# A fused attention and mixture-of-experts kernel: normalisings move from VectorE to ScalarE, lo parts from GpSimd to VectorE, and short chains are laid around the row maxima

## The reference

```python
# x: 16 x 512 x 512, ctx: 16 x 512 x 1024, 16 heads of 32
k, v = split(ctx, 2, axis=2)
q = layernorm(x) * 32 ** -0.5
w = softmax(q_heads @ k_heads.T + b + mask(lens))
x1 = x + tanh(g_xattn) * (w @ v_heads)

z = layernorm(x1)
gates = softmax over the top 2 of 8 of (cosine(z, centroids) + z @ w_route.T)
h = gelu(z @ w1[e] + b1[e])                       # for the 8 experts
x2 = x1 + tanh(g_ffn) * sum_e gates[e] * (h @ w2[e] + b2[e])
```

## Time and profile before

| what | value |
|---|---|
| time, median of 3 runs | 2116.63 us (2108.9 to 2117.64) |
| the profiled execution: its own time | 2109.41 us |
| its span | 2107.5 us |
| PE busy | 1874.4 us, 89% |
| DVE busy | 1521.0 us, 72% |
| ACT busy | 1123.6 us, 53% |
| POOL busy | 652.6 us, 31% |
| mean granted TensorE clock | 0.97 |

### The profile page before, as it was taken

One profiled execution on the slowest core, in us unless ns is written; L12 is line 12 of the kernel. 1 busy time (PEld: TensorE's weight loads), 2 busy tenths in 40 slices (PEclk: granted clock), 3 DMA queues, 4 the chain that ended last, 5 costly groups with the idle time before them and its releaser, 6 DMA issues. The chain is left out here.

```text
span 2107.5 us, 38543 instructions
## 1 busy us (share of the span) xinstructions
PE 1874.4 (89%) x10720; PEld 1050.3 (50%) x10721; DVE 1521.0 (72%) x3639; ACT 1123.6 (53%) x2044; POOL 652.6 (31%) x547
## 2 busy tenths in 40 slices
PE   0599999999999999999999999999459898998987
PEld 0344444444444444444444444444347777777775
DVE  6578788877878777787787787874366666666665
ACT  0165556556555564655655556565145555555554
POOL 1112112111111111211111111210057777777776
PEclk9999999999999999999999999999679999999999
DMA  3877777777876777776887777772348877887774
GB/s 110 134 121 154 115 177 144 136 158 118 187 146 125 156 118 172 141 139 147 134 182 141 130 155 125 154 136 92 124 88 155 145 152 133 159 143 135 140 149 71
DMA packets 173114, 292.01 MB, mean 139 GB/s; under 512 B 37982, under 2 KB 42078, under 8 KB 172944
## 3 DMA queue, kind: packets, MB, share of 16 engines
q1 hardware_dynamic: 140016, 222.26, 52.1%
q0 software_dynamic: 32928, 67.68, 18.4%
HBM read 127.09 MB, written 71.63 MB: 94 GB/s over the span
## 5 line engine op out<-in xcount | busy, mean ns | idle before, releaser
L918 DVE TENSOR_REDUCE mx<-bank 128x1 f32<-128x512 f32 x1024 | 692.8, 685 | 240.2 <-PE bank L714 225.0
L622 ACT ACTIVATE prob<-bank 128x512 f32<-128x512 f32 x1024 | 577.7, 595 | 484.7 <-PE bank L702 484.6
L590 POOL TENSOR_TENSOR regrouped_then_w<-regrouped_then_w 128x512 fp32r<-128x512 f32 x128 | 165.3, 1291 | 1146.6 <-ACT regrouped_then_w L612 1146.6
L714 PE MATMUL bank<-stA,stB 98*128 98x512 f32 x1024 | 427.4, 420 | 71.2 <-DVE mx L918 42.1
L702 PE MATMUL bank<-stB,stA 100*128 100x512 f32 x1024 | 467.5, 459 | 9.1 <-issue 8.8
L702 PEld LDWEIGHTS bank<-stB,stA 100*128 100x128 f32 x1024 | 196.4, 193 | 207.9 <-ACT prob L622 117.0
L675 PE MATMUL bank<-prob,vin 128*32 128x512 f32 x2048 | 279.0, 617 | 0.0
L675 PE MATMUL bank<-prob,ones 128*32 128x512 f32 x2048 | 278.6, 617 | 0.0
L714 PEld LDWEIGHTS bank<-stA,stB 98*128 98x128 f32 x1024 | 202.5, 198 | 117.5 <-DVE mx L918 72.0
L1184 POOL DMA_INDIRECT out_dram<-yout,scatter_ids x144 | 227.8, 1582 | 53.4 <-issue 53.4
L1116 PE MATMUL bankb<-w_hi,gelu_parts 128*128 x576 | 199.4, 407 | 47.9 <-DVE gelu_parts L1358 47.9
(11 more groups left out here) (184 smaller groups left out, 2162.3 us busy)
## 6 DMA issues: line engine op xcount, KB each, us to landing
stB<-regrouped_then_w SPq DMA_DIRECT2D x192, 256.0 KB, 5.7
stA<-regrouped_then_w SPq DMA_DIRECT2D x192, 256.0 KB, 8.4
x_k_then_w<-in_x_dram SPq DMA_DIRECT2D x16, 1024.0 KB, 6.5
x_k_then_w<-in_ctx_dram SPq DMA_DIRECT2D x16, 1024.0 KB, 9.1
vin<-in_ctx_dram SPq DMA_DIRECT2D x16, 1024.0 KB, 6.3
xres<-in_x_dram SPq DMA_DIRECT2D x16, 1024.0 KB, 14.1
xn_rows<-xn SPq DMA_DIRECT2D x64, 256.0 KB, 2.3
out_dram<-xres SPq DMA_DIRECT2D x16, 1024.0 KB, 10.2
```

The costliest lines, as they stand in the source:

```text
L590: pool.tensor_tensor(turnedL[:, side, :], turned[:, side, :], turnedH[:, side, :].bitcast(F32), ALU.subtract).then_inc(s_lo, 1)
L622: act.activation(prob[:, u % 2, j, :], psS[j % 2][:, :], ACT.Exp).then_inc(s_exp, 1)
L714: pe.matmul(psM[s % 2][:, :], stB[0:98, g, j, i * P:(i + 1) * P], stA[0:98, g, j, :], start=True, stop=True).then_inc(s_m, 1)
L918: dve.tensor_reduce(mx[:, s // 4, s % 4:s % 4 + 1], psM[s % 2][:, :], AX.X, ALU.max).then_inc(s_mx, 1)
```

## The change

`turned` and POOL's subtraction go. ACT copies each turned tile once, rounded, and DVE subtracts it from the bank itself (`lo_part`, slots 1 and 5). Both normalisings become ACT instructions with scale and bias from SBUF, each with one more short DVE operation for the bias (`shift`, `shift2`): that of Q in slots 7, 9, 12 and 14 of the step with g 0, that of x1 one step later than before, in slot 8. Turning x1 moves to slot 10 and the routing product to slot 14. The multiplication by tanh(g_xattn) is folded into the addition to `xres`, and the scaling is done in place in the PSUM bank. The two chains for 1/sqrt are put two operations to a slot, one on either side of the maximum: `row_scale` in slots 0 to 8 of the step with g 1, `scale` in slots 5 to 12 of the step with g 3. Column aggregation moves to slots 14 and 15, the statistics of x to steps with g 2 and 3. SP loads `xres` at the end of its step rather than ahead of the rows.

```diff
-TURNS = [("TQ", 3), ("XT", -5), ("MT", 1), ("TK", 3), ("DT", -1), ("OT", -1), ("LG", -5)]
+TURNS = [("TQ", 3), ("MT", 1), ("TK", 3), ("DT", -1), ("OT", -1), ("XT", -5), ("LG", -5)]
...
 SP
-                        if st.on(0):
-                            ...
-                            sp.dma_start(xres[:, par, :, :], x_d[bass.ds(b, 1)]...).then_inc(s_res[par], 16)
...
-                    if st.on(-4):
-                        sp.wait_ge(s_xn2, st.count(1, -4, 1))
+                    if st.on(-5):
+                        sp.wait_ge(s_xn2, st.count(1, -5, 1))
...
+                    if st.g() == 0 and st.on(0):
+                        ...
+                            sp.wait_ge(s_xn2, st.count(1, -4, 0))
+                        sp.dma_start(xres[:, par, :, :], x_d[bass.ds(b, 1)]...).then_inc(s_res[par], 16)
...
 POOL
-                    if st.on(3):
-                        for side, name in ((0, "TQ"), (1, "TK")):
-                            ...
-                            pool.tensor_tensor(turnedL[:, side, :], turned[:, side, :], turnedH[:, side, :].bitcast(F32),
-                                               ALU.subtract).then_inc(s_lo, 1)
...
 ACT
+                def normalise(st):
+                    i, par, half = st.g(-5), ((st.l + 3) // 4) % 2, (st.l + 1) % 2
+                    act.wait_ge(s_ln2, st.batch(LN2, -5, ROW_READY))
+                    ...
+                    act.activation(xn2[:, half, :], xres[:, par, i, :], ACT.Identity, bias=shift2[:, i:i + 1],
+                                   scale=rsb[:, i:i + 1]).then_inc(s_xn2, 1)
+                def normalise_q(st, i):
+                    ...
+                    ins = act.activation(xg[:, i, :].rearrange("p (g c h) -> p g h c", g=NG, h=HG),
+                                         xin[:, par, i, :].rearrange("p (g h c) -> p g h c", g=NG, h=HG),
+                                         ACT.Identity, bias=shift[:, par, i:i + 1], scale=rstd[:, par, i:i + 1])
...
-                    act.activation(turned[:, side, :], bank[:, :], ACT.Copy).then_inc(s_full, 1)
-                    act.activation(turnedH[:, side, :], bank[:, :], ACT.Copy).then_inc(took, 1)
+                    act.activation(turnedH[:, side, :], bank[:, :], ACT.Copy).then_inc(s_full, 1)
...
+                        if s == 8 and st.on(-5):
+                            normalise(st)
+                        if s == 11 and st.on(-5):
+                            bank, took = take_turn(act, st, "XT")
+                            ...
+                        if st.g() == 0 and s in (7, 9, 12, 14) and st.on(4):
+                            normalise_q(st, (7, 9, 12, 14).index(s))
...
 PE
-                        if s == 1 and st.on(-5):
+                        if s == 10 and st.on(-5):
                             pe.wait_ge(s_xn2, st.count(1, -5, 1))
                             bank, done = put_turn(pe, st, "XT")
...
-                        if s == 9 and st.on(-5):
+                        if s == 14 and st.on(-5):
                             b, before = turn_of(st, "XT")
...
 DVE
+                def row_scale(st, k):
+                    c = lambda k: st.batch(LN2, -5, k)
+                    if k == 0:
+                        dve.wait_ge(s_ln2, c(6))
+                    if k < RSQRT_STEPS:
+                        rsqrt(dve, rsb[:, :], rst[:, :], varb[:, :], s_ln2, lambda k: c(6 + k), k, k + 1)
+                        return
+                    ...
+                def lo_part(st, side):
+                    dve.wait_ge(s_full, st.count(2, 3, side + 1))
+                    bank, took = take_turn(dve, st, "TK" if side else "TQ")
+                    dve.tensor_tensor(turnedL[:, side, :], bank[:, :], turnedH[:, side, :].bitcast(F32),
+                                      ALU.subtract).then_inc(took, 1)
...
                     for s in range(16):
+                        if st.g() == 1 and s <= 8 and st.on(-5):
+                            row_scale(st, 2 * s)
+                        if st.g() == 3 and 5 <= s <= 12 and st.on(5):
+                            scale(st, 2 * (s - 5))
                         if st.on(2):
                             ... the maximum of slot s
+                        if s == 0 and st.on(-6):
+                            route_logit(st, s)
+                        if st.g() == 1 and s <= 8 and st.on(-5):
+                            row_scale(st, 2 * s + 1)
+                        if st.g() == 3 and 5 <= s <= 12 and st.on(5):
+                            scale(st, 2 * (s - 5) + 1)
-                        if st.g() == 0 and 1 <= s <= 4 and st.on(4):
-                            normalise_q(st, s - 1)
...
+                        if s in (1, 5) and st.on(3):
+                            lo_part(st, s // 5)
...
-                            dve.tensor_scalar(rsum[:, :, :], rsum[:, :, :], tanh_a[:, 0:1], None, ALU.mult).then_inc(s_rsum, 1)
...
-                            dve.tensor_tensor(scaled[:, :, :]..., bank[:, :]..., each, ALU.mult).then_inc(took, 1)
+                            dve.tensor_tensor(heads, heads, each, ALU.mult).then_inc(s_scaled, 1)
...
-                            dve.tensor_tensor(dst, dst, scaled[:, :, :], ALU.add).then_inc(s_x1a, 1)
+                            dve.scalar_tensor_tensor(out=dst, in0=bank[:, :]..., scalar=tanh_a[:, 0:1],
+                                                     in1=dst, op0=ALU.mult, op1=ALU.add).then_inc(took, 1)
...
-                    if st.on(-4):
-                        if st.g() == 0:
-                            ln2(st, 16)
-                        normalise(st)
```

More of the change, by code:

```diff
@@ L234, in flamingo_kernel @@
             kg = w2a[:, NT * D:2 * NT * D].rearrange("p (i d) -> p i d", i=NT)
[L235 to L236 removed]
+            turnedH, turnedL = [w2a[:, 2 * NT * D + 2 * S * t:2 * NT * D + 2 * S * (t + 1)].rearrange("p (a s) -> p a s", a=2)
+                                        for t in range(2)]
             turnedH, turnedL = turnedH.bitcast(F32R), turnedL.bitcast(F32R)
@@ L624, in step @@
                             evac_turned(st, s // 4)
-                        if s == 1 and st.on(-5):
-                            bank, took = take_turn(act, st, "XT")
-                            act.activation(xT[:, :, :].rearrange("p k t -> p (k t)"), bank[:, :], ACT.Copy).then_inc(took, 1)
                         if s == 3 and st.on(1):
@@ L641, in step @@
                             act.activation(dst[:, (st.l + 1) % 2, :], src[:, :], ACT.Copy).then_inc(s_out, 1)
+                        if s == 8 and st.on(-5):
+                            normalise(st)
+                        if s == 11 and st.on(-5):
+                            bank, took = take_turn(act, st, "XT")
+                            act.activation(xT[:, :, :].rearrange("p k t -> p (k t)"), bank[:, :], ACT.Copy).then_inc(took, 1)
+                        if st.g() == 0 and s in (7, 9, 12, 14) and st.on(4):
+                            normalise_q(st, (7, 9, 12, 14).index(s))
                         if s == 10 and st.g() == 1 and st.on(-6):
@@ L722, in step @@
                             turn_rows(st, s // 4)
-                        if s == 1 and st.on(-5):
-                            pe.wait_ge(s_xn2, st.count(1, -5, 1))
-                            bank, done = put_turn(pe, st, "XT")
-                            for k in range(KD):
-                                last = pe.transpose(bank[:, k * P:(k + 1) * P], xn2[:, (st.l + 1) % 2, k * P:(k + 1) * P], ident[:, :])
-                            last.then_inc(done, 1)
                         if s == 3 and st.on(1):
@@ L742, in step @@
                             last.then_inc(done, 1)
-                        if s == 9 and st.on(-5):
+                        if s == 10 and st.on(-5):
+                            pe.wait_ge(s_xn2, st.count(1, -5, 1))
+                            bank, done = put_turn(pe, st, "XT")
+                            for k in range(KD):
+                                last = pe.transpose(bank[:, k * P:(k + 1) * P], xn2[:, (st.l + 1) % 2, k * P:(k + 1) * P], ident[:, :])
+                            last.then_inc(done, 1)
+                        if s == 14 and st.on(-5):
                             b, before = turn_of(st, "XT")
@@ L809, in ln2 @@
                         dve.reciprocal(nrm[:, 2, :], nrm[:, 1, :]).then_inc(s_ln2, 1)
-                def normalise(st):
-                    i, par = st.g(), ((st.l + 4) // 4) % 2
-                    dve.wait_ge(s_ln2, st.batch(LN2, -4, LN2))
-                    if st.rnd is not None or st.l - 4 >= 2:
-                        dve.wait_ge(s_xns[st.l % 2], st.pair(16, -4, 0))
-                    dve.tensor_scalar(xn2[:, st.l % 2, :], xres[:, par, i, :], mvb[:, i, 0:1], rsb[:, i:i + 1],
-                                      ALU.subtract, ALU.mult).then_inc(s_xn2, 1)
```

142 lines of the change are left out of this document (72 added, 70 removed).

## The result

| what | before | after |
|---|---|---|
| time, median | 2112.92 us (2108.90 to 2117.64) | 2054.91 us (2054.68 to 2057.13) |
| the profiled execution / its span | 2109.41 / 2107.5 us | 2054.78 / 2052.4 us |

What follows compares the result with a forecast made beforehand. PE was taken as nearly the bound, at 20.26 us a free step. Gains of 61.4 us in the loop, 6.8 and 3.8 outside, less 1, gave 71: profiled 2109.4 to 2038, median 2040, range 2024 to 2062.

Steps and rivals of the forecast that it cites:

- rival B: DVE late around slot 9: in-place scaling and addition cost 0.86 us, 0.3 us a step, time 2060; chance 0.14.
- The two stalls: Late maxima in steps with g 0 and where g 1 begins: both go, 3.98 us × 12 batch elements = 47.8 us.
- It is part of the 3.98 us, not extra: Wait for stA rows in steps with g 0, 5.7 us: removing it adds no gain beyond the stalls'.
- The 'issue' wait … stays: PE's wait where the loop body begins anew, five times: stays at 8.8 us, plus 8.5 us of half clock.
- I cost this at nothing: SP's new load order: stack rows come sooner, though the step is 4 us shorter; no cost counted.
- The clock behind the stalls: Stretches at half clock behind the DVE stalls in the loop go, a gain of 18.4 us.
- Load on DVE: About no change per step; lateness around slots 8 and 9 costs 1 us for the whole kernel, bound 19 us.
- Rival A: Lo part of K, on DVE, is held under POOL's K copy: 41 us less gain, time 2081; chance 0.05.
- Rival C: ACT alternating exponential and Identity loads tables at each change: 192 us net, time 2230; chance 0.03.
- Rival D: The loop's beginnings no longer bring half clock: 8.5 us more gain, time 2031; chance 0.1.
- my reason: PE's turnings cost 0.44 us behind a plain product, 0.39 behind a PV; moving two loses 4.8 us.
- The tail and the first steps: Outside the loop: 3.2 and 0.6 us gained in the tail, 6.8 us in two more batch elements.

Runs made afterwards that it cites:

- e4: Kernel before with only the multiplication by tanh folded into the addition to xres: 2090.10 us, ratio 0.9893.
- e9: Kernel before with the tanh multiplication folded into the addition and xres loaded at the end of SP's step: 2077.71 us, ratio 0.9848.
- e10: Kernel before with only the lo parts moved to DVE and ACT copying each turned tile once: 2108.55 us, ratio 0.9988.
- e3: Kernel before with the store of the normalised tile moved behind the loads of x and K, so these precede the jump: 2118.13 us, ratio 1.0037.
- e2: Kernel after with x loaded at the end of SP's step with g 0 and K at the end of that with g 1: 2035.05 us, ratio 0.9637.
- e1: Kernel after with the loads of x and K held until the logits of the step before are done: 2052.41 us, ratio 0.9716.
- e7: Kernel after with a loop body of 16 steps in place of 8: 2031.84 us, ratio 0.9622.
- e8: Kernel after with x and K loaded in separate steps away from the jump and a body of 16 steps: 2027.88 us, ratio 0.9605.
- e11: Kernel after with x and K loads spread, a body of 16 steps, and the turning of x1 one slot later, behind a PV product: 2038.29 us, ratio 0.9667.
- e5: Kernel after with the lo parts taken back: ACT copies each turned tile twice and POOL subtracts: 2064.24 us, ratio 0.9780.
- e6: Kernel after with Q normalised by ACT without the permutation, so the attention is not the reference's: 2056.68 us in one execution.

## Why the prediction was right, and where it was off

**The number: inside the range, by luck in part.** 2054.91 us lies in 2024 to 2062 and outside the 2030 to 2050 that I gave to my own forecast. The upper end is rival B's, a late DVE, and that didn't come. What filled the place up to it was a cost that no rival named.

**The two stalls: right.** 47.8 us were to go; PE's wait for maxima is gone, and between jumps three steps of four take 20.37 us, within 0.01 of the predicted floor of 20.36; the fourth, with g 3, takes up to 20.56, and these 0.13 to 0.19 us, twelve times, are the 1 us or so that I took for DVE's lateness, and a little more. e4, e9 and e10 show that it took the parts together: the fold frees the K copy's place (e4), SP's order frees the rows that come next (e9), and the lo parts pay only once the normalising of Q has left DVE (e10). "It is part of the 3.98 us, not extra" was right for the rows, in the earlier trace rows; that they would become the longer wait once the maxima were gone, had SP's order not changed, the prediction did not say.

**"The 'issue' wait … stays": the term that failed.** I took it over unchanged, 8.8 us and 8.5 us for the clock. It is 20.5 and 13.3, and that is 16.5 of the loop's shortfall of 16.8 us. The prediction had the cause in hand: "it reaches the loads of x and K half a step earlier, over a step whose DMA share is low" and "I cost this at nothing". I asked only whether the rows would come late, and not what else stands in the DMA engines' queues at that moment. e3 shows the size in the kernel before (8.8 to 22.9 us), e2 in the kernel after (20.5 to 7.1), e1 that the fetch of each engine counts, and e7 that it goes with the number of jumps.

**The clock behind the stalls: right in the event, not shown as caused.** I took 18.4 us for half clock behind DVE's stalls. In the trace after, half clock stands at the jumps alone, as forecast. But e3 has none away from its jumps either, and 37.9 us of stalls for maxima. So the stalls don't bring half clock each time, and how much of the 18.4 us the change itself gave back is open.

**Load on DVE: right.** PE has no new wait in slots 10 to 13, so rival B is out (its weight loads wait in slot 13, 3.3 us in all); the operations that no row had shown cost 0.70 and 0.74 us, of the bounds 0.54 and 0.86.

**ACT: price wrong, conclusion right.** 0.59 us for a normalising came from a copy out of PSUM. It costs 0.80, and 1.32 with the permutation. ACT is 657.88/48 = 13.7 us a step where I wrote less than 12.7, and it had the room. At the start it had not: four normalisings in front of the first product take 4.42 us together, 2.40 on DVE before, 2.0 more, and the first part is 1.8 us longer.

**Rival A: false for its victim.** The lo part of K is not held, and neither is the inversion, both with a PSUM operand. **Rival C: false.** Still two table loads in the whole run, one in the setup and one in the expert part, 1.28 us each; identity alternates with the exponential in every step. **Rival D**, a clock kept after the loop's beginnings, didn't come with the kernel after; e2 and e8 come close to it, once the loads are moved.

**PE: the sum right, its reason not shown.** Slot 10 takes 0.93 and slot 14 1.35 us, 0.46 and 0.88 more than a plain one. The step's sum came out within 0.01 us. By my reason a turning behind a PV is cheaper. e11 moved one there and lost 0.1 us a step, but it took slack from DVE at the same time, so it doesn't tell the price by itself.

**The tail and the first steps: undersized.** 3.51 us a tile and 6.2 us in all against 3.69 and 3.8; steps −2 to 7 gained 6.9 us and not half of it, and the waits for rows in them, which I had not counted, fell from 7.7 to 5.6 us together, and 3.4 us of half clock at 192.8 us are gone. The rest of both I haven't split.

**Still open.** The expert part isn't touched, and is 585.6 us long after 582.6 before. In the eleven experiments it lies between 582.6 and 589.1 with no order that I can see. At 3 to 6 us it is as large as the effects above in e5 and e11, and I can't say what sets it.

## What to carry to other kernels

Where an engine's loop body begins anew, look at what the DMA engines are doing: bulk loads that are under way there are paid in instruction fetch on every engine that jumps meanwhile, and then in clock; put them in the middle of the body, one at a time, or make the body longer. If a step of a queue is moved, ask what it will run beside, even where nothing waits for its data. And when a stall has been hiding others (rows behind maxima, a normalising behind a multiplication), do one part alone to see which comes next: the whole change was worth 58 us, and its lo parts alone nothing.

## What the runs showed of the hardware

- A jump to the start of the loop costs PE 1.3 to 2.1 us of issue wait where no large load was issued ahead of it (before, e2, e4, e8 to e11), and 4.0 to 4.7 with 2 MB of loads under way (after, e3, e5, e6). DVE, where it jumped beneath the loads, waited 5.6 to 6.5 us (e1, e7). With the long wait the clock was at 0.50 for 6.8 us nearly each time, beginning at most 1.8 us before PE went on; with the short one not at all or for 3.4 us, and once, in e8, for 6.8.
- A DVE TENSOR_SCALAR from SBUF to SBUF waits for a POOL operation under way: 4.51 us for one of 0.77, e10; 1.27 for one of 0.16, e5. With one operand in PSUM DVE doesn't wait: 0.68 and 0.26 us under a copy of 4.07. Nor do all that read and write SBUF alone: BATCH_NORM_AGGREGATE took its 0.18 us under a subtraction, e5.
- ACT reading SBUF with scale and bias from SBUF takes 0.80 us for 128x512, 0.21 more than a copy from PSUM, and 1.32 where the elements that it writes lie 16 bytes apart.
